# A graph network on one core: own rows transposed into the bank of the edge sums

## The reference

```python
# gcn, twice (128 -> 256 -> 128); deg counts the edges and adds one more self-loop
msg = h[src] * (dinv[src] * dinv[dst])
out = segment_sum(msg, dst) + b          # src, dst with a self-loop added: own rows count twice
# sage, three times
agg = segment_sum(h[src], dst) * inv_deg
# attention and a GRU
att = sigmoid(xs @ W_att[:d] + xd @ W_att[d:] + b_att)
aggregated = segment_sum((xs @ W_msg + b_msg) * att, dst)
r, z = sigmoid(i_r + h_r), sigmoid(i_z + h_z)
n = tanh(i_n + r * h_n)
h_new = (1 - z) * n + z * x              # then a batch norm over all nodes
# last layer
neigh @ W_neigh.T + b_neigh + x @ W_self.T + b_self
```

## Time and profile before

| | us |
|---|---|
| median of three timed runs | 5293.26 |
| the profiled execution | 5291.49 |
| its span | 5289.7 |
| TensorE busy / weight loads | 4562.4 / 3502.8 |
| VectorE busy | 3617.5 |
| GpSimd busy | 3012.8 |
| ScalarE busy | 2700.3 |

### The profile page before, as it was taken

One profiled execution on the slowest core, in us unless ns is written; L12 is line 12 of the kernel. 1 busy time (PEld: TensorE's weight loads), 2 busy tenths in 40 slices (PEclk: granted clock), 3 DMA queues, 4 the chain that ended last, 5 costly groups with the idle time before them and its releaser, 6 DMA issues. The chain is left out here.

```text
span 5289.7 us, 103008 instructions
## 1 busy us (share of the span) xinstructions
PE 4562.4 (86%) x26356; PEld 3502.8 (66%) x26356; DVE 3617.5 (68%) x11417; ACT 2700.3 (51%) x6655; POOL 3012.8 (57%) x2949
## 2 busy tenths in 40 slices
PE   4499996666699989999999997888789999888777
PEld 4478885565466656676767765777656666777777
DVE  8567776766566645555555554788668888876776
ACT  2645555767444442222222222777777777674555
POOL 0077775777677755444444443777476666007776
PEclk9999998888799999999999998999999999999999
DMA  4889995666599985545455452788777777784554
GB/s 149 286 243 285 285 283 180 196 197 198 194 328 324 328 303 168 172 163 173 163 170 168 165 173 95 234 243 247 235 233 234 238 230 226 258 311 144 151 152 140
DMA packets 576023, 1145.99 MB, mean 217 GB/s; under 512 B 114083, under 2 KB 121034, under 8 KB 572810
## 3 DMA queue, kind: packets, MB, share of 16 engines
q1 hardware_dynamic: 475802, 924.73, 51.4%
q0 software_dynamic: 100080, 219.67, 16.1%
HBM read 705.95 MB, written 438.05 MB: 216 GB/s over the span
## 5 line engine op out<-in xcount | busy, mean ns | idle before, releaser
L881 POOL DMA_INDIRECT s_rows<-t_h,s_index x417 | 520.8, 1249 | 714.0 <-DVE s_index L874 614.9
L881 POOL DMA_INDIRECT g_rows<-t_x,g_index x417 | 417.5, 1001 | 375.5 <-issue 362.4
L881 POOL DMA_INDIRECT cb_rows<-t_x,cb_index x417 | 396.1, 950 | 381.3 <-DVE cb_index L874 256.3
L881 POOL DMA_INDIRECT at_rows<-t_m,at_index x417 | 442.0, 1060 | 270.1 <-DVE at_index L874 160.9
L881 POOL DMA_INDIRECT s_rows<-t_v,s_index x417 | 405.8, 973 | 203.8 <-issue 122.0
L881 POOL DMA_INDIRECT s_rows<-t_x,s_index x417 | 420.5, 1008 | 151.2 <-issue 121.4
L1805 ACT ACTIVATE s_hid<-bank,sb_c 128x512 f32<-128x512 f32 x196 | 124.1, 684 | 730.6 <-PE bank L1778 730.6
L881 POOL DMA_INDIRECT g_rows<-t_h,g_index x417 | 404.0, 969 | 161.8 <-issue 126.3
L947 PE MATMUL bank<-g_onehot,g_rows 128*128 128x168 f32 (+4 forms) x980 | 241.1, 408 | 198.3 <-DMA g_rows<-t_h,g_index 198.1
L1842 DVE TENSOR_TENSOR s_rout<-bank,s_x 128x512 f32<-128x512 f32 x98 | 67.8, 691 | 491.4 <-PE bank L1790 491.4
L947 PE MATMUL bank<-s_onehot,s_hi 128*128 128x168 f32 (+4 forms) x1470 | 351.1, 282 | 57.0 <-DVE s_lo L915 52.1
(11 more groups left out here) (356 smaller groups left out, 12695.5 us busy)
## 6 DMA issues: line engine op xcount, KB each, us to landing
s_scale<-inv_d SPq DMA_DIRECT2D x196, 256.0 KB
htt<-s_ht SPq DMA_DIRECT2D x98, 512.0 KB
t_h<-s_hout SPq DMA_DIRECT2D x98, 512.0 KB
s_ht<-htt SPq DMA_DIRECT2D x98, 512.0 KB
t_m<-s_mout SPq DMA_DIRECT2D x98, 264.0 KB
at_own<-t_m SPq DMA_DIRECT2D x98, 264.0 KB
t_x<-so_x SPq DMA_DIRECT2D x98, 256.0 KB, 4.4
g_own<-t_x SPq DMA_DIRECT2D x98, 256.0 KB
```

Of the source, the lines that this page charges most:

```text
L881: pool.indirect_dma_start(out=self.rows[:, self.row(q, k), :], out_offset=None, in_=self.table[0:NPAD, :], in_offset=bass.IndirectOffsetOn ...
```

## The change

`gcn_first` and `attend` no longer multiply own rows with a scaled identity. They transpose them into the bank, with the bank's first write, and the edge products accumulate on top. As a transpose can't scale, the factor moves to ScalarE: in `gcn_first` a new operation multiplies the own rows by `own1` in place (`raise_own`, after `take_hi` in ScalarE's queue), and the sums wait for it in place of the load; in `attend` the four attention weights of each partition are multiplied by `own` in place, between the sigmoid and the weighings, with a wait on its result (semaphore `kept_own`). `id_own1`, `id_own` and their two operations go, and so does an unused tile.

```diff
-                dve.tensor_scalar(id_own1[:, :], ident[:, :], own1[:, 0:1], None, ALU.mult)
-                dve.tensor_scalar(id_own[:, :], ident[:, :], own[:, 0:1], None, ALU.mult)
...
+    def turn_into(pe, to, rows):
+
+        for b in range(BLK):
+            pe.matmul(nodes(to)[:, b, :], rows(b), ident[:, :], start=(b == 0), stop=False, is_transpose=True,
+                      skip_group_check=True)
...
                     e.fetched(pe, q)
-                    pe.wait_ge(loaded[q.u], q.n * 16 + 16)
+                    pe.wait_ge(raised, q.t + 1)
                     if not is_first(q.t):
                         pe.wait_ge(agged, q.t - 1)
-                    e.sum_by_feature(pe, q, [bank[q.u]], close=False)
-                    for b in range(BLK):
-                        last = pe.matmul(nodes(bank[q.u])[:, b, :], own_rows[q.u][:, b * D:(b + 1) * D],
-                                         id_own1[:, :], start=False, stop=(b == BLK - 1),
-                                         skip_group_check=True)
-                    last.then_inc(e.summed, 1)
+                    turn_into(pe, bank[q.u], lambda b: own_rows[q.u][:, b * D:(b + 1) * D])
+                    e.sum_by_feature(pe, q, [bank[q.u]], open_=False).then_inc(e.summed, 1)
...
-                over_groups(act, [(4, relu), (6, scale), (0, lambda q: e.take_hi(act, q))])
+                def raise_own(q):
+                    act.wait_ge(loaded[q.u], q.n * 16 + 16)
+                    act.activation(own_rows[q.u][:, :], own_rows[q.u][:, :], ACT.Copy, scale=own1[:, 0:1])\
+                       .then_inc(raised, 1)
+
+                over_groups(act, [(4, relu), (6, scale), (0, lambda q: e.take_hi(act, q)), (0, raise_own)])
...
                     pe.wait_ge(mailed, q.t + 1)
                     if not is_first(q.t):
                         pe.wait_ge(agged, q.t - 1)
-                    e.sum_by_feature(pe, q, [bank[q.u]], close=False)
-                    for b in range(BLK):
-                        last = pe.matmul(nodes(bank[q.u])[:, b, :], mine[q.u][:, b, :],
-                                         id_own[:, :], start=False, stop=(b == BLK - 1),
-                                         skip_group_check=True)
-                    last.then_inc(e.summed, 1)
+                    turn_into(pe, bank[q.u], lambda b: mine[q.u][:, b, :])
+                    e.sum_by_feature(pe, q, [bank[q.u]], open_=False).then_inc(e.summed, 1)
...
                     act.activation(att[q.u][:, :], logit[q.u][:, :], ACT.Sigmoid).then_inc(weighed, 1)
                     act.wait_ge(weighed, q.t + 1)
+                    act.activation(att[q.u][:, :], att[q.u][:, :], ACT.Copy, scale=own[:, 0:1]).then_inc(kept_own, 1)
+                    act.wait_ge(kept_own, q.t + 1)
                     if not is_first(q.t):
                         act.wait_ge(e.summed, q.t - 1)
```

More of the change, by code:

```diff
@@ L225, in build_program @@
     dcol = sb("dcol", [P, SLOTS])
-    dsg = sb("dsg", [P, SLOTS])
     dinv_n = sb("dinv_n", [P, T * BLK])
@@ L235, in build_program @@
     own1 = sb("own1", [P, 1])
-    id_own1 = sb("id_own1", [P, P])
-    id_own = sb("id_own", [P, P])
     bn_acc = sb("bn_acc", [P, T + BLK - 1, 6])
@@ L936, in fetched, with sum_by_feature @@
             pe.wait_ge(self.ready, q.t + 1)
-        def sum_by_feature(self, pe, q, banks, close=True):
+        def sum_by_feature(self, pe, q, banks, open_=True, close=True):
             todo = pieces(q.r)
@@ L947, in sum_by_feature @@
                         last = pe.matmul(to[:, a:b], part[:, at, h * P:(h + 1) * P],
-                                         self.onehot[:, self.place(q, k), off:off + b - a], start=(i + s == 0),
+                                         self.onehot[:, self.place(q, k), off:off + b - a],
+                                         start=(open_ and i + s == 0),
                                          stop=(close and i + 1 == len(todo) and s + 1 == len(sources)),
@@ L1413, in gcn_first @@
             agged, relued, scaled, rested = ph.sem("agged"), ph.sem("relued"), ph.sem("scaled"), ph.sem("rested")
-            hidden, lowered, link = ph.sem("hidden"), ph.sem("lowered"), ph.sem("link")
+            hidden, lowered, link, raised = ph.sem("hidden"), ph.sem("lowered"), ph.sem("link"), ph.sem("raised")
             st_h, st_r = ph.sems("stored_h"), ph.sems("stored_r")
@@ L2018, in attend @@
             loaded_x, loaded_m = ph.sems("loaded_x", XS), ph.sems("loaded_m")
-            opens, weighed = ph.sem("opens"), ph.sem("weighed")
+            opens, weighed, kept_own = ph.sem("opens"), ph.sem("weighed"), ph.sem("kept_own")
             gated, mailed, agged = ph.sem("gated"), ph.sem("mailed"), ph.sem("agged")
```

## The result

The changed kernel takes 5304.61 us (median of 20 runs, 5292.19 to 5319.45), the kernel before on the same chip 5290.28 (20 runs, 5280.67 to 5302.53). The ratio is 1.0029, with a 95% interval of 1.0022 to 1.0036: 0.29% slower (the medians are 14.3 us apart), just within the 0.3% that were called no change, though the interval reaches beyond it. The profiled execution took 5301.95 us with a span of 5300.1; the one before has a span of 5289.7. So the two spans, 10.4 us apart, show most of the difference.

A forecast was written before the change was run, and what follows sets the result against it. GpSimd's gathers were taken to bound `gcn_first` and a store circuit `attend`, hiding TensorE's gain. From the profiled 5291.5: +10.1 - 1.5 - 0.4 = 5299.7, say 5300 us; own range 5293 to 5307, two in ten outside 5276 to 5322.

The forecast's parts named there:

- the circuit: `attend`: loop through ScalarE, SyncE, the store's DMA landing and VectorE, without TensorE; about 6.9 us a group, sets the pace.
- TensorE, both stages: `gcn_first` and `attend`: four transposes (0.43 us) replace eight passes (0.97), 0.54 us a group less, hidden by GpSimd and the circuit.
- The rival that TensorE sets the end: Both stages: TensorE, busy 100 of 100 us, is the bound, so the time falls to 5186 us; 4 in 100.
- raise_own: `gcn_first`: new ScalarE operation of 0.66 us, 98 times, covered by VectorE's `take_lo`; costs nothing, or 65 us without cover.
- the rival of late rows in `gcn_first`: Own rows' load lands too late once `raise_own` takes 0.66 us of its room; slower, 5340 us; 5 in 100.
- The end of `gcn_first`, and `sort_and_scale`: Last group's sums end sooner, -1.5 us (bounds 0 and 1.9); two operations dropped from a serial chain, -0.4 us.
- The scaling of `att`: `attend`: added ScalarE operation and wait inside the circuit, 0.22 us a turn, +10.1 us (8.7 to 14.3).
- the 46 turns of the forecast: `attend`: the circuit closes 46 times, each turn covering two groups, nearly the whole stage.
- the last rival: Added operation costs more (0.35 us a turn, 5306 us), or counts in every group (5311 us); 10 in 100.
- The clock: Both stages: TensorE's new pauses lower its granted clock, deciding below 0.90; slower, 5329 us; 8 in 100.
- GpSimd quicker: `gcn_first`: gathers fall from 1.005 us towards `combine`'s 0.949, up to 23 us, 5276 us; 12 in 100.

The follow-up runs named there:

- before_4g: Kernel before, with the fifth gather of every fourth group in `gcn_first` left out from the ninth group on: 5290.64 us, ratio 0.9997.
- after_4g: Changed kernel, with the fifth gather of every fourth group in `gcn_first` left out from the ninth group on: 5276.80 us, ratio 0.9973.
- no_scale: Changed kernel, with the factor on `att` given as a bias column of the existing sigmoid, not an added operation: 5299.63 us, ratio 1.0003.
- no_scale_hn: no_scale with three buffers for new h in place of two and a semaphore per store: 30 us faster than the kernel before, `attend` 668.5 us.
- g1_only: Changed kernel with `attend` put back to its products, so only `gcn_first` is changed: 5299.26 us, ratio 1.0001.
- imm: Changed kernel, with the added operation on `att` kept but scaled by the constant 1.0, not a column: 5310.03 us, ratio 1.0026.
- after_hn: Changed kernel with three buffers for new h in place of two and a semaphore per store: `attend` 686.0 us, 28.5 us shorter.
- open_order: no_scale_hn with `gate` before `weigh` in ScalarE's queue in `attend`: 5272.60 us, ratio 0.9968.
- at_only: Changed kernel with `gcn_first` put back to its scaled identity, so only `attend` is changed: 5321.30 us, ratio 1.0045.

## Why the prediction was right, and where a term was off

**Forecast 5300, measured 5304.61; against 5290.28 before, +0.27% where +0.13% was forecast.** The sign, the place and the mechanism came out: nothing in `gcn_first`, a loss in `attend` by an operation in the circuit. The size did not: the change is 14.3 us where 6.7 was forecast, about twice as much. The absolute time flatters the forecast by 3.0 us, as it was reckoned from three runs with a median of 5293.3, and twenty have 5290.3.

**TensorE, both stages.** Forecast 0.43 us for four transposes, hidden in both stages. Measured 0.36 to 0.41, hidden in both: 93 of 100 us busy. The reason in `gcn_first`, GpSimd, is shown by the pair `before_4g` and `after_4g`; that in `attend` by `no_scale`, which is relieved of the products, has no added operation and is still no faster than the kernel before, until `no_scale_hn` takes the store away. The rival that TensorE sets the end, and with it 5186 us, falls: TensorE was relieved by some 7 of 100 us in both stages, and the time did not fall. The Trainium skill, page "Perfetto Trace Analysis", section "Identifying the Most-Contended Engine", would have the engine with the highest occupancy improved first, TensorE judged by its weight loads. In `gcn_first` these were the highest, 82.24 of 100 us and 72.39 after, and the stage is no shorter, so the measurement goes against the rule there. In `attend` they were 64.43, below VectorE's 84.74, so there the rule doesn't name TensorE at all, which the prediction overlooked.

**`raise_own`.** Forecast 0.66 us each, covered. Measured 0.707, and 1.0 us of waits for it. It has a column and L903 of the earlier trace rows has none; whether that makes the excess was not tried. ScalarE waited 13 times, 10.0 us in all, for own rows in this stage and made TensorE late by no more than that 1.0 us; the rival of late rows in `gcn_first` falls.

**The end of `gcn_first`, and `sort_and_scale`.** Forecast -1.5 and -0.4 us. The end of the stage came 4.3 us earlier in the profile after, but 5.0 later in that of `g1_only`, which has the same `gcn_first`. These two terms are smaller than the scatter of one profile, and neither is shown or refuted.

**The scaling of `att`: the term that was mis-sized.** Forecast 0.22 us a turn, 10.1 us; bounds 0.19 to 0.31, 8.7 to 14.3 us. Measured 0.33 a turn, above the upper bound, and `attend` longer by 19.3 us. By the table it makes up so, with the 46 turns of the forecast: 0.33 for the operation, 0.06 from `move` to `blend`, 0.02 in the landing of the store, together 0.41 x 46 = 18.9. Only the 0.33, or 15.2 us, is firm; over all five profiles with either `attend` the turn grows by 0.36 (13.86 to 14.22 in the mean), or 16 us, near to the 14.3 of the medians. This is the first half of the last rival, the added operation that costs more, which had 0.35 us a turn and 5306. The step that failed is the choice of the nearest row. The sigmoid has the same shape and the same wait, but no operand that is a column of SBUF, and the added operation has one. The weighings have such a column, and so were the nearer row; the 0.31 that I took from their pitch as the upper bound is 0.30 by the trace, four operations of 0.386 us starting within 1.28. A pitch without a wait between was no bound either, as the added operation has a wait for its own result: 0.22 with the wait and 0.09 for the column is 0.31, and the Copy takes 17 ns longer than the sigmoid (206 to 189), which makes 0.33. The 0.06 from `move` to `blend` may be scatter, as `after_4g` has 0.02 of it. `blend` waits for `z` from ScalarE there (19.8 us in 29 waits after, 15.3 in 29 before), and ScalarE's gates are later by the added operation too; that this adds anything was not tested.

**The clock.** The rival had the pauses bring the clock down. TensorE pauses in each group now, and the windows of the two stages show 1.00 in the profile after. That is not the whole record: from 300 to 800 us five of the eight kernels with transposes in `gcn_first` show 0.99 (`g1_only`, `no_scale`, `imm`, `after_hn`, `open_order`), and none of the four with products does. The profile after has a short dip too:

```profile
355.00:365.00 10.00, 7.89 (x45) 6.89 (x46) 7.84 (x22) 5.72 (x12) 7.56 (x9) 0.83 0.80 240
```

0.83 is a mixture of the two levels, with TensorE busy for 7.89 of 10 us. So the rival's effect exists, at a hundredth where it needed a tenth (0.90) to decide, and no stage length follows it: `no_scale` has 0.99 and 562.2 us, the kernel before 1.00 and 563.9. The Trainium skill, page "TensorE: Matmul & The Clock Gate", section "Part 4: PE-mode transpose", has transposes not count as products do, which spoke for the rival. Whether the pauses or the transposes bring the 0.99, no run here shows. The mean clock over the span is 0.931 in the profile after and 0.954 before, but that comes from another place (below).

**GpSimd quicker.** A gather takes 996 ns where it took 1005; the rival wanted down to 949. It is worth 0.009 x 417 = 4 us at most, which the scatter hides.

**From the sum to the median.** The span grew by 10.4 us and not by 19.3, since the other stages came out 8.6 us shorter ahead of `attend` in that one profile; in the medians it is 14.3. The forecast is thus nearer to the time than its largest term was to its stage.

**What is left open.** `gcn_first` alone measures 1.0001 and `attend` alone 1.0045, the whole 1.0029: the parts add up to somewhat more than the whole, mostly as `at_only`'s stores land later (4.38 against 4.22 us). The intervals of `at_only` and the whole overlap (1.0032 to 1.0059 and 1.0022 to 1.0036), so it may be nothing, and I have no cause for the landing.

## What to carry to other kernels

An engine at 100% is a bound only if nothing runs beside it at the same pace: in both stages a second limit (GpSimd's gathers; a circuit through a reused buffer, a store's landing and an in-order queue) stood within some 0.1 us a group of it, so that in `attend` the transposes without the added operation moved nothing, the third buffer alone moved nothing, and the two together brought 30 us. Before work is moved to an engine with room, ask whether its place there is in a circuit, since an idle share says nothing on that. And price an added operation by a row with the same kinds of operands, not only the same shape and the same wait.

## What the runs showed of the hardware that I had not expected

A column of SBUF as scale or bias costs ScalarE 91 to 93 ns, which makes an operation of 128x4 nearly half as long again (206 to 297, 189 to 282 ns).

The granted clock at the start differs between executions whose work there is the same. From 0 to 240 us, first the kernel before, then the one after:

```profile
0.00:240.00 240.00, 116.89 (x1660) 112.40 (x1660) 187.24 (x306) 120.19 (x392) 6.08 (x30) 1.00 0.68 221
```

```profile
0.00:240.00 240.00, 116.84 (x1660) 112.47 (x1660) 186.67 (x304) 121.80 (x394) 6.07 (x30) 0.54 0.68 220
```

0.54 is near the 1.2 GHz level throughout, 1.00 is 2.4 GHz; yet TensorE's busy time is the same for the same 1660 instructions. It makes up the fall of the mean clock over the span, from 0.954 to 0.931, and has nothing to do with the change. `after_hn` and `before_4g` have 0.54 there too (117.02 and 116.93 us busy), the other nine profiles, with the kernel before, 1.00. It is a matter of the single execution: of the twenty runs of the changed kernel six have a mean clock of 0.928 to 0.931 and fourteen 0.952 to 0.957, with medians of 5304.7 and 5304.6 us, and of the 66 runs of the kernel before beside the experiments nine have 0.929 to 0.933. What decides it I can't say.
